# Products of ones in TensorE's waits, the ternary normalisation on ScalarE, and the last feed-forward block spread over its neighbour

## The reference

```python
x = x + tanh(g_xattn[0]) * L0_xattn(layernorm(x), ctx, ...)   # attention over 77 context tokens, 16 heads
x = x + tanh(g_ffn[0])   * L0_ffn(layernorm(x), ...)          # 8 experts, top 2, and a shared expert
x = x + tanh(g_xattn[1]) * L1_xattn(layernorm(x), ctx, ...)   # attention, then a feed-forward net, two layer norms
x = x + tanh(g_ffn[1])   * L1_ffn(layernorm(x), ...)          # ternary weights, below

def L1_ffn(x):
    h = layer_norm(x, ln1_g, ln1_b)
    h = gelu(h @ ternary_quant(w1).T + b1)        # 256 -> 1024
    h = layer_norm(h, ln2_g, ln2_b)
    return h @ ternary_quant(w2).T + b2           # 1024 -> 256
```

## Time and profile before

| | us |
|---|---|
| median of 3 runs | 1276.95 (1276.65 to 1279.39) |
| the profiled execution | 1286.48 |
| its span, first to last instruction | 1284.7 |
| TensorE busy | 1200.1 |
| VectorE busy | 1004.2 |
| ScalarE busy | 771.0 |
| GpSimd busy | 660.6 |

### The profile page before, as it was taken

How to read it: one execution, slowest core, us unless ns; L and a number is a source line. 1 busy time by engine, 2 the same in 40 slices (tenths; PEclk the granted TensorE clock), 3 DMA queues, 4 the chain that set the end, 5 groups by cost and what they waited for, 6 DMA issues and landing times.

```text
span 1284.7 us, 27101 instructions
## 1 busy us (share of the span) xinstructions
PE 1200.1 (93%) x9168; PEld 1106.7 (86%) x9169; DVE 1004.2 (78%) x2107; ACT 771.0 (60%) x1487; POOL 660.6 (51%) x755
## 2 busy tenths in 40 slices
PE   7999999979888999999799999999999998799997
PEld 6888888879778999999688888888899997678877
DVE  6888888857797767675768888886987876888886
ACT  4777677657554555555557777676344545467663
POOL 5333333333104555563877777631554654578786
PEclk9999999989999999999869999999999999899999
DMA  3222111023201333343533333302000000000000
GB/s 102 55 65 57 51 51 51 19 65 110 72 1 48 115 98 111 102 111 101 112 63 60 60 61 61 60 23 93 23 2 0 0 0 1 1 26 25 24 24 33
DMA packets 72317, 68.66 MB, mean 53 GB/s; under 512 B 26624, under 2 KB 64256, under 8 KB 72000
## 3 DMA queue, kind: packets, MB, share of 16 engines
q1 hardware_dynamic: 57936, 47.78, 12.6%
q0 software_dynamic: 12576, 18.62, 7.8%
q10 hardware_dynamic: 1744, 1.50, 0.5%
HBM read 44.00 MB, written 18.61 MB: 49 GB/s over the span
## 4 chain that ended last, share of the span: by engine, by line
PE 75%; DVE 11%; issue 6%; ACT 5%; POOL 2%; DMA 0%; ACTq 0%; DVEq 0%; POOLq 0%
PE PSUM L771 13%; PE PSUM L773 12%; PE PSUM L772 12%; PE PSUM L831 6%; PE PSUM L852 6%; PE PSUM L840 4%; PE PSUM L784 3%; PE PSUM L850 2%; PE PSUM L2725 2%; PE PSUM L2726 2%; PE PSUM L807 2%; PE PSUM L861 1%; PE PSUM L2717 1%; PE PSUM L2706 1%; PE PSUM L2705 1%
## 5 line engine op out<-in xcount | busy, mean ns | idle before, releaser
L2157 POOL TENSOR_TENSOR s_f_h_lo<-s_f_h,s_f_h_hi 128x512 fp32r<-128x512 f32 x64 | 90.8, 1427 | 108.2 <-ACT s_f_h_hi L2107 107.7
L1336 POOL DMA_INDIRECT s_m_tile_x<-normed_x,s_tokens x78 | 95.7, 1227 | 76.7 <-DVE s_tokens L1627 55.2
L852 PEld LDWEIGHTS PSUM<-s_a_v_diagonal,s_a_prob_t 128*128 128x128 f32 x1024 | 128.4, 195 | 0.0
L852 PE MATMUL PSUM<-s_a_v_diagonal,s_a_prob_t 128*128 128x36 f32 x1024 | 127.4, 271 | 0.0
L1004 POOL DMA_INDIRECT s_x<-sorted_y,s_slots x60 | 95.2, 1587 | 51.1 <-DMA s_x<-sorted_y,s_slots 34.5
L453 DVE TENSOR_REDUCE s_a_row_max<-PSUM 128x8 f32<-128x640 f32 x128 | 104.4, 816 | 13.7 <-PE PSUM L831 10.8
L701 ACT ACTIVATE s_a_prob_t<-PSUM 128x640 f32<-128x640 f32 x128 | 89.5, 700 | 34.2 <-PE PSUM L840 33.4
L831 PE MATMUL PSUM<-s_a_kd,s_a_q_hi 64*128 64x320 f32 x512 | 92.8, 366 | 16.7 <-DVE s_a_q_lo L421 16.3
L460 DVE TENSOR_TENSOR s_a_less<-PSUM,s_a_row_max 128x640 f32<-128x640 f32 x128 | 105.0, 820 | 3.6 <-issue 0.2
L684 ACT ACTIVATE s_a_prob<-s_a_less 128x512 f32<-128x512 f32 x128 | 80.5, 629 | 42.1 <-DVE s_a_less L460 42.0
L2101 ACT ACTIVATE s_f_h<-PSUM,s_cols 128x512 f32<-128x512 f32 x64 | 44.1, 688 | 91.0 <-PE PSUM L773 87.4
(11 more groups left out here) (314 smaller groups left out, 4298.3 us busy)
## 6 DMA issues: line engine op xcount, KB each, us to landing
sorted_y<-s_m_tile_y SPq DMA_DIRECT2D x39, 256.0 KB, 2.1
s_a_kd<-s_a_k_parts SPq DMA_DIRECT2D x252, 20.0 KB
s_x<-x SPq DMA_DIRECT2D x16, 256.0 KB, 2.8
s_a_ctx<-ctx SPq DMA_DIRECT2D x32, 128.0 KB, 2.5
s_moe_raw<-moe_w SPq DMA_DIRECT2D x16, 256.0 KB, 3.4
normed_x<-s_m_xn SPq DMA_DIRECT2D x16, 256.0 KB, 3.2
y<-s_x SPq DMA_DIRECT2D x16, 256.0 KB, 2.1
s_late_raw<-moe_w SPq DMA_DIRECT2D x11, 256.0 KB, 2.9
```

The lines of the kernel that those rows point to most:

```text
L852: last = pe.matmul(a.o_ps[:, 2 * c:2 * c + 2, :], a.prob_t[j % 2][:, c, :], v[:, j // BT, 0, 2 * c:2 * c + 2], start=False, stop=c == PC - ...
L1336: pool.indirect_dma_start(m.tile_x[n % 2][:, t, :], None, d["normed_x"], bass.IndirectOffsetOnAxis(ap=tokens[:, BT * n + t:BT * n + t + 1] ...
L2157: pool.tensor_tensor(f.h_lo[m % 4][:], f.h[m % 4][:], f.h_hi[m % 4][:].bitcast(F32), ALU.subtract).then_inc(f.h_split, 1)
```

## The change

It has three parts.

1. `turn_over(pe, bank, n)` issues n products of ones (128x512, fp32r) into a PSUM bank that is free, and nobody reads them. They stand ahead of waits of TensorE: 3 and 7 at the entry of attention 0 (with 8 transposes of the identity before them), 2, 6 and 5 at its end, 4, 13, 2 and 7 in the mixture ahead of the second products of shared blocks 5, 6, 8 and 9, and 4, 12 and 7 at the entry of attention 1: 72 in all.
2. `ternary_norm` moves from VectorE to ScalarE, as x * rstd + shift; GpSimd works out shift = -mean * rstd in two further small instructions. The statistics of a block are now taken two blocks ahead, and `ternary_inverse_std` stands at the end of a block's tile 3 instead of in its tile 0. ScalarE's loop over ternary blocks is written out.
3. The last feed-forward block's statistics, scaling and addition to x are spread over the first ternary block's tiles on VectorE and GpSimd; GpSimd adds the output bias to x ahead (`f_x_biased`), so that VectorE does one pass less. The last ternary tile is worked in halves of 512 channels, its multiplication on VectorE, its last products into a PSUM bank of their own.

```diff
+        def turn_over(pe, bank, n):
+            for _ in range(n):
+                pe.matmul(bank.rearrange("p (r n) -> p r n", n=P), ones_r[:], ones_r[:].unsqueeze(1).broadcast_to([P, 4, P]),
+                          start=True, stop=True)
...
             if a.stage == 0:
                 pe.wait_ge(pool_const, CONSTS)
-            pe.wait_ge(consts_done, 1)
+                for _ in range(8):
+                    pe.transpose(PSUM[:, 0, 0:P], ident[:], ident[:])
+            pe.wait_ge(first_steps, 1)
+            if a.stage:
+                turn_over(pe, PSUM[:, 0, :], 4)
             open_scores()
...
-                keys(first).then_inc(first_keys, 1)
+                keys(first).then_inc(first_steps, 1)
+                turn_over(pe, a.first_x_bank, 3)
...
                 last_of_mixture(ALL - 1)
+                pe.wait_ge(a.v_main, a.base + 1)
+                pe.wait_ge(a.v_tail, a.base + 1)
+                turn_over(pe, a.misc, 12)
                 transpose_x(first)
...
             pe.wait_ge(a.v_ones, a.stage + 1)
+            turn_over(pe, PSUM[:, 5, :], 7)
...
             def shared_down(b):
+                after(pe, m.y_done, b.n)
+                turn_over(pe, PSUM[:, 4, :], {5: 4, 6: 13, 8: 2, 9: 7}.get(b.n, 0))
                 pe.wait_ge(m.h_split, b.n + 1)
-                after(pe, m.y_done, b.n)
...
         def ternary_inverse_std(pool, w, b):
             pool.wait_ge(w.ln_stats, b.count + 1)
-            pool.tensor_tensor(w.rstd1[:], w.var1[:], neghalf[:, 0:MT], ALU.pow).then_inc(w.ln_rstd, 1)
...
+            pool.tensor_tensor(w.rstd1[:], w.var1[:], neghalf[:, 0:MT], ALU.pow)
+            pool.tensor_tensor(w.less_mean1[:], w.mv1[:, :, 0], minus_one[:, 0:MT], ALU.mult).then_inc(w.ln_mean, 1)
+            pool.wait_ge(w.ln_mean, b.n + 1)
+            pool.tensor_tensor(w.shift1[:], w.less_mean1[:], w.rstd1[:], ALU.mult).then_inc(w.ln_rstd, 1)
...
-        def ternary_norm(dve, w, b):
-            dve.wait_ge(w.ln_rstd, b.count + 1)
+        def ternary_norm(act, w, b):
+            act.wait_ge(w.ln_rstd, b.count + 1)
...
+                last = act.activation(w.xn[:, t, :], x[:, MT * b.n + t, :], ACT.Identity, scale=w.rstd1[:, t:t + 1],
+                                      bias=w.shift1[:, t:t + 1])
...
+                    if t == 0 and not behind:
+                        last_stats()
+                    if t == MT - 1 and not ahead:
+                        last_tile(b)
+                        continue
...
+                    if t == 1 and not behind:
+                        last_scale()
...
+                    if t == 2 and not behind:
+                        last_sum()
+                    if t == 2 and ahead > 1:
+                        ternary_stats(dve, w, b.next().next())
+                    if t == 3 and ahead > 1:
+                        ternary_aggregate(dve, w, b.next().next())
```

More of the change, by code:

```diff
@@ L972, in attention_on_tensor @@
                 ffn_up(1)
+            else:
+                turn_over(pe, PSUM[:, 5, :], 2)
             transpose_o(final, 0)
@@ L2122, in body @@
                         ternary_rows_on_scalar(act, w)
+                    if m == 3 and not ahead:
+                        ternary_norm(act, w, ternary_first)
                     if m >= HC - KC and not ahead:
@@ L2259, in body @@
                     sums(b.last())
+                    stats_2(b.last())
+                if not ahead:
+                    ternary_stats(dve, w, ternary_first)
                 if ahead:
@@ L2265, in body @@
                     aggregate_2(b.last(), ahead)
+                if not ahead:
+                    ternary_aggregate(dve, w, ternary_first)
                 if ahead:
@@ L2271, in body @@
                 if behind:
-                    apply_2(b.last())
+                    scale_2(b.last())
+                    shift_2(b.last())
+                if behind:
                     residual(b.last())
@@ L2533, in body @@
                         bias_laid(t)
-                    if t == 2 and ahead:
-                        x_affine(act, w, b.next(), 0)
                     if t >= 1:
@@ L2539, in body, with ternary_on_gpsimd @@
                         rounded(b.last(), MT - 1)
-            paired_blocks(act, MB, body, w.base)
-            rounded(Block(MB - 1, 1, (MB - 2) // 2, w.base), MT - 1)
+                    if t == 0 and ahead and behind:
+                        ternary_norm(act, w, b.next())
+                    if t == 2 and ahead:
+                        x_affine(act, w, b.next(), 0)
+            for n in range(MB):
+                body(Block(n, n % 2, n // 2, w.base), n > 0, n < MB - 1)
+            last_rounded()
         def ternary_inverse_std(pool, w, b):
             pool.wait_ge(w.ln_stats, b.count + 1)
-            pool.tensor_tensor(w.rstd1[:], w.var1[:], neghalf[:, 0:MT], ALU.pow).then_inc(w.ln_rstd, 1)
-        def ternary_on_gpsimd(pool, w):
+            after(pool, w.ln_done, b.count if not isinstance(b.n, int) or b.n else 0)
+            pool.tensor_tensor(w.rstd1[:], w.var1[:], neghalf[:, 0:MT], ALU.pow)
+            pool.tensor_tensor(w.less_mean1[:], w.mv1[:, :, 0], minus_one[:, 0:MT], ALU.mult).then_inc(w.ln_mean, 1)
+            pool.wait_ge(w.ln_mean, b.n + 1)
+            pool.tensor_tensor(w.shift1[:], w.less_mean1[:], w.rstd1[:], ALU.mult).then_inc(w.ln_rstd, 1)
+        def ternary_on_gpsimd(pool, w, last_norm_of_ffn):
             def scale_h(b, t):
@@ L2661, in body @@
                         ternary_residue(dve, w, b.next())
+                    if t == 0 and not behind:
+                        last_stats()
+                    if t == MT - 1 and not ahead:
+                        last_tile(b)
+                        continue
                     stats_2(b, t)
-                    if t == 0 and ahead:
-                        ternary_stats(dve, w, b.next())
+                    if t == 1 and not behind:
+                        last_scale()
                     if t >= 1:
@@ L2668, in body @@
                         residue(b.last(), MT - 1)
-                    if t == 1 and ahead:
-                        ternary_norm(dve, w, b.next())
+                    if t == 1 and not behind:
+                        rows()
                     if t >= 2:
@@ L2743, in body @@
                         ternary_transpose(pe, w, b.next(), 1)
-                    up(b, t)
+                    up(b, t, not ahead and t == MT - 1)
                     if t == 1 and not behind:
                         rows()
+                    if t >= 1:
+                        transpose_h(b, t - 1)
+                    elif behind:
+                        transpose_h(b.last(), MT - 1)
                     if t == 2 and ahead:
```

182 lines of the change are left out of this document (126 added, 56 removed).

## The result

Over 20 runs of each in turn the changed kernel takes 1271.05 us (1265.30 to 1278.13) and the kernel before 1279.18 (1275.68 to 1287.22). The ratio is 0.9929, with a 95% interval of 0.9911 to 0.9947: 8 us less, not 24.8. The profiled execution of the changed kernel takes 1273.84 us, its span is 1272.1 and its mean clock 0.981. For the kernel before these are 1286.48, 1284.7 and 0.976.

What follows compares the result with a forecast made beforehand. TensorE, busy 93% of the span, was taken as the bound, with clock dips and waits for VectorE. Gains 3.0 + 1.0 + 2.5 + 3.4 + 11.0 + 2.5 + 1.4 = 24.8 from 1276.95 gave 1252.5 us, range 1243 to 1263.

Steps and rivals of the forecast that it cites:

- Rival 1: The clock gives nothing back and only the reordering works: 1262 us; chance 0.17.
- Rival 4: Gains at the seam are given back by ScalarE as the ternary loop's new bound: 1275 us; chance 0.04.
- Part 1, entry of attention 1: Twelve and seven products fit into waits of 3.56 and 2.11 us; slow time from 624 to 640 gives back 3.4.
- Rival 3: The products stand on the path; if all 72 meet no wait, 33 us are added: 1285 us; chance 0.04.
- Part 1, the start: At attention 0's start the products bring TensorE's clock up earlier: 3.0 us gained, bounds 4.3 gained and 1.4 lost.
- rival 5: The start stays slow, as small products and transposes do not raise the clock: 3.0 less, 1255.5 us; chance 0.10.
- Part 1, the mixture: Products raise the clock at the mixture's entry, 1.0 us gained, and at two places inside it, 2.5 gained.
- these 9 us: Slow stretch from 640 to 672 us in attention 1, counted against the profiled execution's 1286.48, not the median 1276.95.
- Part 3, the seam: From last feed-forward block to ternary net: earlier transposes and no slow stretch, 11.0 us gained, bounds 7 and 13.5.
- Given back later ... 1.3: Behind the seam VectorE owes block 7's last pass and statistics, so block 1's `s_t_x_lo` is late: 1.3 us lost.
- Part 2, the loop: Ternary blocks lose the 1.13 us wait but gain two smaller ones: 2.5 us gained over seven blocks.
- The signs named: Right: fast early transposes, clock 1.00 near 340 and 618, no ternary-entry wait over 2 us, shorter blocks; wrong: products delaying awaited work.

Runs made afterwards that it cites:

- no_products: The changed kernel without its 8 first transposes, all 72 products of ones and the two waits ahead of the twelve; 1270.12 us, ratio 0.9923.
- only_products: The kernel before with the transposes and 72 products alone, no norm on ScalarE and no reordering; 1281.35 us, ratio 1.0012.
- in_waits: The changed kernel with attention 1's twelve products ahead of their waits, and seven, five and ten more at both attentions and the mixture's first logits; 1272.76 us.
- lo_before_stats: The changed kernel with the last feed-forward sum in tile 3 of ternary block 0 and `x_lo` ahead of the statistics in every ternary block; 1274.15 us.
- sum_later_in_wait: The changed kernel with the last feed-forward sum in tile 3 and attention 1's twelve products ahead of their waits; 1264.24 us, ratio 0.9876.

## Why the prediction was wrong

The range ended at 1243 and 1263, and 1271.05 lies 8 us above it. Rival 1 (1262) had the mechanism nearest, since the products give nothing back in the times. Rival 4's number (1275) is closer, but what it gave as the reason, ScalarE as the loop's new bound, is not what the traces show: the loop got shorter. By runs, two terms failed. The products were to give 9.9 us and give 0 (1271.05 with them, 1270.12 without). The reordering was to give 14.9 and gives 9.0. A further 2.2 us are in the base: the sum was taken from 1276.95, the median of three runs, and over 20 runs before has 1279.18.

**Part 1, entry of attention 1** (the step "Twelve (2.8 us) fit into 3.56"). This is the step that failed most. The length of the wait was right, the place was not. The diff has two waits ahead of the twelve, for the readers of the bank that they write, and what they wait for ends 0.7 us ahead of what the transposes wait for. A wait that is behind the products would have hidden them; this one is in front. Forecast 3.4 gained; in the traces with the twelve behind the waits 3.6 to 4.5 are lost between 604 and 622 us in seven and 1.1 in one, where the level was up, and in those with them ahead of the waits or left out between 0.8 lost and 1.2 gained. Rival 3 had the mechanism, but only for products that meet no wait at all.

**Part 1, the start.** "Gives back 4.3 at most, I take 3.0": the mechanism holds in every profile with these products (1.0 to 4.9 us ahead at 27 us), and rival 5 is out. In the eleven with the change's start, what is left at 60 us is 1.2 on the mean (from 2.5 to -1.1) instead of 3.0: the wait of 1.81 us for VectorE takes part of it, and in some there is a new dip behind it.

**Part 1, the mixture.** Neither its entry (1.0) nor the two places (2.5) gave anything: from 60 to 604 us the profiles with the change's products lose up to 1.7 us (one gains 0.2), those with ten more at the logits gain 0.0, 1.5 and 2.4, and no_products gains 0.3. The dip at 368 went in the change's profile, but eleven of the 15 profiles with the products have 3.4 us at the lower level at 365 to 377 us, as before has. In the change's profile VectorE is busy for 15.33 of 16 us there, as it was before (15.38), which leaves little to gain.

**The clock as a whole.** The mean clock did rise, from 0.9805 to 0.9854, worth 4.5 us by the slope. The entry's loss takes it back: at equal clock the change is 3.6 us faster than before (0.9 either way), no_products 8.2 (1.6), and only_products 4.7 slower (1.2). These add up. That rows of one execution showed a dip did not mean that others have it there; the profile of before had 20.4 us from 640 that no_products does not have either (8.8 us gained from 622 to 670 without a product). I had set these 9 us aside, which fits: of the other 16 profiles only two have a dip over 10.3 us there (in_waits 20.5, lo_before_stats 13.7). No second profile of before was taken. The prediction also counts dips in three of 40 slices of the earlier trace rows; the line shows four, which changes no term.

**Part 3, the seam.** 11.0 forecast, 7.6 to 8.6 measured. The transposes came within 1.4 us of the forecast and the slow stretch gave 3.1, not 2.5. The term that was off is "Given back later ... 1.3": it is 3.9 (3.0 to 3.9 over the profiles with this order), since `x_lo` stands behind 3.0 us of VectorE's work and then meets GpSimd's multiplication.

**Part 2, the loop.** 2.5 forecast. From block 2 to the end the profiles of the change's order gain 3.7 to 3.9, of which the end has 1.3 (1.4 forecast), so the loop has 2.5. The waits are those that were named. TensorE's timeline of after, two blocks:

```profile
1164.03 1.09 PE L2838 MATMUL PSUM<-s_ident,s_t_gh 128*128 128x128 f32 x8 [0.81 <-POOL s_t_gh L2636]
...
1172.76 0.66 PE L2810 MATMUL PSUM<-s_ident,s_t_xn 128*128 128x128 f32 x4 [0.68 <-ACT s_t_xa L2549]
...
1194.30 0.66 PE L2810 MATMUL PSUM<-s_ident,s_t_xn 128*128 128x128 f32 x4 [0.37 <-ACT s_t_xa L2549]
```

One block takes 21.54 us instead of 22.1. What the forecast lacked is block 2's meeting, 3 us in most profiles. Seam, meeting, loop and end make 9.8 to 10.1 or 12.7 to 13.3 us, 11.2 on the mean of eight profiles; by the medians of the runs it is 9.0, by the fit at equal clock 8.2. The rest of that difference is open: before has its own dip from 1104 in the profile, which may be absent in other runs of it. The one other profile with before's order there, only_products, has it too (10.2 us from 1099).

**The signs named.** Two signs of being right came: five transposes at full clock at 21.57 us, and ternary blocks 0.6 us shorter. The clock was below 1.00 at 336 and 624 us, and a wait of 2.65 us stands where the ternary net begins. The first sign of being wrong came at the entry of attention 1: products followed at once by the awaited transposes, later than before.

Also open: why the same order of VectorE gains 14.7 us from 1068 on in sum_later_in_wait and 13.0 and 13.1 in two other profiles, why ten or seven products more bring a long dip in attention, and the dip of some 10 us where attention 1 ends (864 us in the changed kernel), which seven of the profiles have.

## What to carry to other kernels

An operation that is to fill a wait has to stand ahead of it, and may need nothing that the wait is for: look at what it must wait for itself, its output's readers above all, and choose a buffer that is free. Read a dip of the clock from several executions before giving it a price: one profile shows which dips can come, not which do, and kernels that differ by a few instructions show others. Where two blocks' work is pressed into fewer tiles, count the receiving engine's work tile by tile, and look which operation of it will begin beside another engine's long one, and which of the two begins first.
